# Attention kernel: the fold of a round's eight partial maxima moves from VectorE (one reduce) to GpSimd (ten small instructions)

## The reference

```python
dot = jnp.einsum('bqhs,bkhs->bhqk', queries, keys)      # 16 heads, 4096 x 4096
attn = jax.nn.softmax(dot, axis=-1)
out = jnp.einsum('bhqk,bkhs->bqhs', attn, values).reshape(b, t, e)
```

## Time and profile before

| what | value |
| --- | --- |
| runs | 3708.22, 3710.76, 3708.29 us; median 3708.29 us |
| span of the profiled execution, first to last instruction | 3708.1 us |
| VectorE busy in it | 3199.3 us (86%) |
| TensorE busy in it | 3608.8 us (97%) |
| attention rounds | from about 407 us to 2808 us |
| GpSimd busy in it | 367.6 us (10%) |

### The profile page before, as it was taken

The page is one execution under the profiler, slowest core; times in us unless marked ns, Lnnn a source line. Parts: engine busy times, 40 slices in busy tenths (PEclk is TensorE's granted clock), DMA queues, the critical chain, the costliest instruction groups (busy, mean ns, idle before and its releaser), DMA issues. The chain is left out here.

```text
span 3708.1 us, 77955 instructions
## 1 busy us (share of the span) xinstructions
PE 3608.8 (97%) x31342; PEld 2065.1 (56%) x31342; DVE 3199.3 (86%) x4508; ACT 2643.1 (71%) x4950; POOL 367.6 (10%) x329
## 2 busy tenths in 40 slices
PE   7899999999999999999999999999998989999998
PEld 6587544444444444444444444444445668888887
DVE  6656899999999999999999999999975757766664
ACT  2455699888888898888989888989896442223332
POOL 0133100000000000000000000000002203403323
PEclk9899999999999999999999999999999999999999
DMA  4920322022022022112112202211012000122332
GB/s 133 256 41 18 113 21 29 4 30 26 7 23 33 6 21 24 19 9 30 24 7 26 27 6 24 33 7 7 4 31 84 34 2 27 56 97 63 82 85 39
DMA packets 297388, 149.13 MB, mean 40 GB/s; under 512 B 216097, under 2 KB 275559, under 8 KB 294480
## 3 DMA queue, kind: packets, MB, share of 16 engines
q1 hardware_dynamic: 284752, 133.61, 19.5%
q0 software_dynamic: 12288, 10.70, 1.7%
HBM read 86.44 MB, written 63.83 MB: 41 GB/s over the span
## 5 line engine op out<-in xcount | busy, mean ns | idle before, releaser
L1236 ACT ACTIVATE probs<-attention_scores_t_sums 128x512 f32<-128x512 f32 x4096 | 2142.4, 597 | 244.5 <-PE attention_scores_t_sums L1161 241.4
L1161 PE MATMUL attention_scores_t_sums<-q_operand,k_operand 50*128 50x512 f32 x2048 | 703.1, 443 | 7.9 <-ACTq L1251 6.1
L1155 PE MATMUL attention_scores_q_sums<-attention_k_operand,attention_q_operand 48*128 48x512 f32 x2048 | 701.2, 439 | 0.3
L1161 PE MATMUL attention_scores_t_sums<-attention_q_operand,attention_k_operand 50*128 50x512 f32 x2048 | 700.2, 443 | 0.0
L1155 PE MATMUL attention_scores_q_sums<-k_operand,q_operand 48*128 48x512 f32 x1952 | 669.9, 440 | 0.2
L1273 DVE TENSOR_REDUCE max_parts<-attention_scores_q_sums 128x1 f32<-128x512 f32 x1008 | 640.0, 672 | 1.1 <-PE attention_scores_q_sums L1155 1.1
L1273 DVE TENSOR_REDUCE attention_max_parts<-attention_scores_q_sums 128x1 f32<-128x512 f32 x992 | 630.0, 672 | 0.0
L1266 DVE TENSOR_REDUCE max_parts<-attention_scores_q_sums 128x2 f32<-128x1024 f32 x504 | 606.8, 1204 | 5.1 <-PE attention_scores_q_sums L1155 5.0
L1171 PE MATMUL attention_o_psum_sums<-probs,v_heads 128*32 128x256 f32 x8192 | 602.1, 388 | 0.0
L1171 PE MATMUL attention_o_psum_sums<-probs,attention_v_heads 128*32 128x256 f32 x8192 | 600.6, 388 | 0.0
L1266 DVE TENSOR_REDUCE attention_max_parts<-attention_scores_q_sums 128x2 f32<-128x1024 f32 x496 | 598.1, 1206 | 0.9 <-PE attention_scores_q_sums L1155 0.6
(11 more groups left out here) (331 smaller groups left out, 4674.8 us busy)
## 6 DMA issues: line engine op xcount, KB each, us to landing
expert_rows<-attention_empty_rows SPq DMA_DIRECT2D x16, 516.0 KB, 6.1
v_scratch<-value_chunk SPq DMA_DIRECT2D x16, 512.0 KB, 5.4
w_whole<-in_L_ffn_ew SPq DMA_DIRECT2D x8, 1024.0 KB, 6.7
experts_w_whole<-in_L_ffn_ew SPq DMA_DIRECT2D x8, 1024.0 KB, 5.5
q_operand<-q_scratch SPq DMA_DIRECT2D x24, 256.0 KB, 4.8
k_operand<-k_scratch SPq DMA_DIRECT2D x24, 256.0 KB, 6.4
attention_q_operand<-q_scratch SPq DMA_DIRECT2D x24, 256.0 KB, 4.8
attention_k_operand<-k_scratch SPq DMA_DIRECT2D x24, 256.0 KB, 6.6
```

Source lines behind the costliest of these rows:

```text
L1155: nc.tensor.matmul(SA[:, (2 * h + j) * CH:(2 * h + j + 1) * CH], QOP[b][64 * h:64 * h + ROWS, qt * P:(qt + 1) * P], KOP[b][64 * h:64 * h + ...
L1161: nc.tensor.matmul(ST[bank_n][:, :], KOP[b][64 * h:64 * h + ROWS + 2, kt * P:(kt + 1) * P], QOP[b][64 * h:64 * h + ROWS + 2, c * CH:(c + 1 ...
L1236: nc.scalar.activation(PR[:, tile, :], ST[bank_n][:, :], ACT.Exp).then_inc(st_free, 1)
```

## The change

VectorE no longer has `negative_max`. GpSimd does it at the head of `split_max`: in three steps (four, two and one part wide) it computes second minus first, the positive part of that, and adds it to the first, which leaves the maximum of the two; a last subtraction from zero negates it. Each of the ten instructions waits for the one before it. GpSimd starts when `sa_free` says that the round's last partial maximum is written. VectorE waits, ahead of a round's first `reduce_first`, until the parts it will overwrite (those of two rounds before) have been folded.

```diff
-    RECIP_AT = 12
+    RECIP_AT, FOLDS = 12, 10
...
+        OVER = sb("max_excess", [P, 2, 4, 4])
...
-        neg_ready = sem("neg_max_ready")
+        folded = sem("max_parts_folded")
...
+            fold = Chain(pool, folded)
+
+            def negative_max(n, par):
+                pool.wait_ge(sa_free, 4 * (n * U + U - 1) + 8)
+                parts = MPART[par]
+                for w in (4, 2, 1):
+                    first, second, over = parts[:, :, :, 0:w], parts[:, :, :, w:2 * w], OVER[:, :, :, 0:w]
+                    fold(nc.gpsimd.tensor_tensor(over, second, first, ALU.subtract))
+                    fold(nc.gpsimd.tensor_scalar(over, over, 0.0, None, ALU.max))
+                    fold(nc.gpsimd.tensor_tensor(first, first, over, ALU.add))
+                fold(nc.gpsimd.tensor_tensor(NEG[:, :, :], ZERO[:, :, :], parts[:, :, :, 0], ALU.subtract))
+
             def split_max(n, par):
-                pool.wait_ge(neg_ready, n + 1)
+                negative_max(n, par)
                 pool.wait_ge(max_out, 16 * (n + 1))
...
             def reduce_first(par, u, s):
                 first = 2 * (u % 4)
+                if u == 0 and s >= 3 * U:
+                    dve.wait_ge(folded, FOLDS * (s // U - 2))
                 dve.wait_ge(sa_ready, 4 * s + 2)
...
-            def negative_max(par, s, splits):
-
-                dve.wait_ge(sa_free, 4 * s + 8)
-                dve.wait_ge(msplit, 2 * splits)
-                nc.vector.tensor_reduce(NEG[:, :, :], MPART[par][:, :, :, :], AX.X, ALU.max, negate=True)\
-                    .then_inc(neg_ready, 1)
...
-                        if s_unit == 0 and not (last and s_round > HALF):
-                            negative_max((s_round - 1) % 2, s - 1, g + (u + LEAD) // U - 1)
```

More of the change, by code:

```diff
@@ L1259, in _ @@
             dve.sem_inc(sa_free, 4 * LEAD + 4)
-            dve.sem_inc(neg_ready, 1)
             tail.normalise(nc, dve, links)
```

## The result

The changed kernel takes 3715.12 us (median of 18 runs, 3712.57 to 3722.54); the kernel of before, over 18 runs of its own, 3711.49 us (3705.07 to 3714.83). The ratio is 1.0015, 95% interval 1.0008 to 1.0021: slower by some 5.6 us, and less than 0.2%. (The medians are 3.6 us apart, the means 5.2.) The forecast was 3709.2 us in a range of 3701 to 3731. Spans of the profiled executions: 3708.1 before, 3713.2 after, 5.1 us apart.

What follows compares the result with a forecast made beforehand. VectorE was taken to set the pace, TensorE following closely. From a span of 3708.1 us, less 7.8 saved on VectorE, plus 8.7 for late rows, came 3709.0; with 0.2 for the median, 3709.2 us, range 3701 to 3731.

Steps and rivals of the forecast that it cites:

- VectorE sets the pace: Attention stretch: VectorE bounds it, TensorE following closely; each fold removed saves 0.126 us, 62 of them 7.8 us.
- The chain: GpSimd's ten dependent instructions before the split: 3.01 us with handovers, so the rows come 1.75 us later.
- Room of 1.8 us with a spread: Between the rows' landing and TensorE's first score tile of the round: 1.8 us taken, standard deviation 0.35 us.
- the forecast's own formula: Lateness of the rows at TensorE: 1.79 us against room of 1.8, spread 0.35, mean 0.14 us, over 62 rounds 8.7 us.
- The sum: Whole kernel: span 3708.1 us less 7.8 saved on VectorE plus 8.7 for late rows, 3709.0 us.
- late in every round: Rival: GpSimd's chain is longer than 3.0 us and the rows late every round; about 3733 us, chance 0.34.
- The rows still arrive in time: Rival: room nearer 3 us or a shorter chain leaves only the gain; 3700.5 us, 0.21% faster, chance 0.10.
- GpSimd slows VectorE: Rival: GpSimd's work slows VectorE's reduces; 3 us a round at 5% would be 9 us, chance 0.01.

Runs made afterwards that it cites:

- experiment 7: The kernel before the change with VectorE's fold done twice, the second time into a tile nobody reads: 3718.01 us, ratio 1.0017.
- experiment 1: The changed kernel without the nine folding instructions on GpSimd, only the subtraction from zero kept: 3697.67 us, ratio 0.9966 to the kernel before.
- experiment 5: The changed kernel with GpSimd folding parts as they come in, six instructions left behind the last reduce: 3701.14 us, ratio 0.9966 to the kernel before.
- experiment 6: The changed kernel with the nine folding instructions left out and three idle additions behind the kept subtraction: 3699.16 us, ratio 0.9968 to the kernel before.
- experiment 3: The changed kernel with four more dependent idle additions at the end of GpSimd's chain: 3837.0 us, ratio 1.0329 to the kernel before.
- experiment 4: The changed kernel with the SP queue issuing the output's stores ahead of the wait for the maximum: 3785.53 us, ratio 1.0217 to the kernel before.
- experiment 8: The kernel before the change with the output's stores issued ahead of the wait for the maximum: 3712.51 us, ratio 1.0002.
- experiment 9: The changed kernel with the SP queue reordered to stores first, then operand loads, row transfers last: 3723.78 us, ratio 1.0037 to the kernel before.

## Why the prediction held, point by point

- *VectorE sets the pace; the fold costs it 0.126 us a round, 7.8 us.* Right. A second fold costs 7.6 us of the stretch (experiment 7), and the unit at the border went from 2.46 to 2.33 us. Taking the only fold away gives 9.7 to 10.2 us (experiments 1, 5, 6), of which 7.9 us stand in the unit at the border, the mechanism as forecast. The other 2 us are spread over the whole round. VectorE's waits for TensorE account for about 1 us of them (3.1 us before, 2.0 us in 6 places in experiments 1, 5 and 6); what the rest is stays open.
- *The chain: 3.01 us, the rows 1.75 us later.* Somewhat short, and this is the term that was mis-sized. The split comes 3.27 us after the last reduce (1560.12 to 1563.39), worked out were 3.09; against 1.33 before it is 1.94 us later. Its parts: `tensor_scalar` took 0.28, 0.25 and 0.24 us where the copy's row had led to 0.245, 0.228 and 0.22, together 0.08 us; the ten handovers took 0.083 us each where 0.077 was put, 0.06; and the three additions ran 0.03 over. The subtractions of 32 and 16 elements came out as worked out (0.25, 0.21).
- *Room of 1.8 us with a spread.* Right. The prediction had only bounds of 1.2 and 3.6 us and chose; the semaphores' times measure it. In the round of its rows the transfers landed at 1570.27 us, 1.46 us ahead of TensorE's 1571.73. Over 62 rounds of the kernel before they landed 1.82 us ahead on average, with a standard deviation of 0.39 us (0.54 at the least). The value within such wide bounds was part judgement, part luck. In the changed kernel TensorE starts within 0.1 us of the landing in 44 of the 62 rounds. With 1.94 us for 1.75 in the forecast's own formula the average round is 0.18 us late, the mean lateness with a spread of 0.35 is 0.25 us, and 62 rounds give 15.4 us. Measured are 14.5 us (experiment 1 against the changed kernel); the forecast had 8.7.
- *The sum.* Forecast -7.8 + 8.7 = +0.9 us; measured -9.7 + 14.5 = +4.8 us in the stretch. The saving was low by 1.9 us and the lateness by 5.8; by the formula, the chain's 0.19 us on a steep slope is enough for the latter. That the time came out near the forecast is in part luck: the 2 us that no term of the sum had offset a third of the missing lateness.
- *The rival "late in every round".* Its mechanism is the one that lost the gain, and it was near: the prediction let it begin at a chain of some 3.2 us, and the chain took 3.19 (first subtraction to split). The lateness came to 14.5 us, where some 15 would have made it. Experiment 3 shows the slope past that point: the lateness itself grows as the rival had it, and what comes in the units behind the gaps makes it steeper.
- *"The rows still arrive in time"* didn't happen here, but in experiment 5, by shortening the tail.
- *GpSimd slows VectorE.* No: in experiment 5 GpSimd has three times the instructions, and there is no loss. The median of the wide reduce is 1204 ns before, 1210 after, and 1208 in experiments 5 and 7, the last with no fold on GpSimd, while the units stay at 2.33 us.

The Trainium skill (GPSIMD Engine Reference, Engine selection) gives reduces along the free dimension to VectorE. For the time of the single operation the trace bears it out: 3.19 us on GpSimd for 0.13 us on VectorE. For the time of this kernel it does not: with VectorE the bound, GpSimd's 29 small instructions a round are 0.34% faster (experiment 5). What decides is whether the result is waited for.

The Trainium skill (the same reference, Performance pitfalls for Q7 kernels) names an extra cycle an element for reads with an inner step over 8 bytes. A one-wide subtraction of 8 elements took 209 ns on average and the split's of 8 contiguous ones 202; the one-wide addition took 220 and the split's contiguous one 204. If that is it, it is 0.01 to 0.02 us an instruction.

## What to carry to other kernels

Moving an operation from the engine that sets the pace to an idle one pays the time between starts, not the record's length. It costs by the length of the dependent chain behind the last input, set against the room at the far end, which has to be measured through every link (here the write, four transfers, the wait of TensorE). With mean room equal to the delay a change still loses by the spread; fold early what is there early, so that only the last input has a tail.

## What the runs showed of the hardware

- A gap of 1.43 us on TensorE in experiment 3 was followed by a stretch of 3.4 us with the granted clock at 0.52, the lower level of 1.2 GHz (the rest is at 2.4), and cost VectorE about as much again as the gap. The changed kernel's gaps, 0.77 us in the round shown and 1.8 us at most, had none of it (granted clock 1.00 from 433 to 2765 us): a single gap as long is not enough, and what else is needed was not tried.
- Loads of 256 KB issued right behind four transfers of 512 elements of four bytes delayed their landing by about 1.3 us, though they were issued later on the same queue (12.9 to 13.5 us after the write in experiment 4, 13.0 to 13.4 in experiment 8, 11.9 with the loads moved ahead in experiment 9); with stores of 1 to 16 KB there it was 11.7.
- Ten dependent instructions of GpSimd on 8 to 32 elements took 3.19 us, 0.29 to 0.37 us each from start to start, and 0.28 to 0.30 us on 2 elements: at these sizes it is the count that costs.
